# The last additions of the first two chunks of tokens: from VectorE to GpSimd

## What is computed

```python
h = h + attention(layernorm(h))
xt = layernorm(h)
shared = silu(xt @ sw1) * (xt @ sw3) @ sw2                  # one expert for every token
idx = top_k(xt @ gate_w.T + biases, 2)                       # two of eight experts for each token
p = sigmoid(top scores) / sum                                # their two weights
y = silu(xt @ w1[e]) * (xt @ w3[e]) @ w2[e]                  # for each token and chosen expert e
out = h + shared + p[0] * y[first] + p[1] * y[second]
```

## Time and profile before

| | |
|---|---|
| median of three runs | 264.31 us (263.71 to 264.48) |
| the profiled execution, whole | 264.31 us |
| its span in the profile | 262.5 us |
| busy: TensorE, VectorE, ScalarE, GpSimd | 89%, 72%, 59%, 44% |

### The profile page before, as it was taken

How to read it: one execution, slowest core, us unless ns; L and a number is a source line. 1 busy time by engine, 2 the same in 40 slices (tenths; PEclk the granted TensorE clock), 3 DMA queues, 4 the chain that set the end, 5 groups by cost and what they waited for, 6 DMA issues and landing times.

```text
span 262.5 us, 5589 instructions
## 1 busy us (share of the span) xinstructions
PE 233.8 (89%) x1491; PEld 192.2 (73%) x1491; DVE 189.9 (72%) x737; ACT 155.3 (59%) x436; POOL 115.2 (44%) x121
## 2 busy tenths in 40 slices
PE   0499799999999999989899957999999999999960
PEld 0477688888879797966566636888888888888640
DVE  1533998798989898987988767766666666665784
ACT  0325458585858585875974325666666666666571
POOL 1400000055646464640656720676666666676600
PEclk9999799999999999997999997999999999999996
DMA  6989964143434301010011412324323332348736
GB/s 199 318 271 338 333 241 149 39 122 126 117 127 121 136 21 44 20 40 2 31 42 50 135 43 52 93 62 113 85 82 91 85 98 75 99 112 236 202 99 181
DMA packets 31421, 31.68 MB, mean 121 GB/s; under 512 B 4322, under 2 KB 27403, under 8 KB 30496
## 3 DMA queue, kind: packets, MB, share of 16 engines
q1 hardware_dynamic: 25960, 23.95, 30.7%
q0 software_dynamic: 3392, 6.36, 7.4%
q10 hardware_dynamic: 2040, 1.04, 1.4%
HBM read 22.80 MB, written 9.03 MB: 121 GB/s over the span
## 4 chain that ended last, share of the span: by engine, by line
PE 80%; DVE 9%; ACT 5%; ACTq 3%; issue 2%; DVEq 0%
PE bank L1565 15%; PE bank L1281 12%; PE bank L1585 10%; PE bank L1296 5%; PE bank L1574 5%; PE bank L1488 3%; PE bank L1473 3%; PE bank L1476 3%; PE bank L1369 2%; PE bank L1556 2%; PE bank L1329 2%; PE bank L1373 2%; PE bank L1295 2%; PE bank L1327 2%; PE bank L1355 2%
## 5 line engine op out<-in xcount | busy, mean ns | idle before, releaser
L778 POOL DMA_INDIRECT xs_dram<-xd,pos_i x50 | 54.9, 1099 | 82.7 <-DVE pos_i L967 69.9
L789 POOL DMA_INDIRECT y_dram<-att,goal x56 | 56.4, 1007 | 37.7 <-ACT att L713 37.4
L1281 PE MATMUL bank<-wt,xp_both 128*128 128x128 f32 x288 | 38.6, 288 | 0.0
L1281 PEld LDWEIGHTS bank<-wt,xp_both 128*128 128x128 f32 x288 | 36.9, 201 | 1.4 <-issue 0.7
L699 ACT ACTIVATE att<-bank 128x256 f32<-128x256 f32 x56 | 21.5, 383 | 24.9 <-PE bank L1565 24.9
L1585 PE MATMUL bank<-w_sb,att 128*128 x224 | 34.5, 277 | 0.0
L1190 DVE CAST xsT_h<-bank 128x128 fp32r<-128x128 f32 x56 | 16.3, 292 | 24.9 <-PE bank L1556 24.9
L1585 PEld LDWEIGHTS bank<-w_sb,att 128*128 128x128 f32 x224 | 29.4, 191 | 0.3 <-issue 0.2
L1565 PE MATMUL bank<-xp_both,xsT_h 128*128 x56 | 27.3, 488 | 1.5 <-DVE xsT_l L1192 1.5
L1203 DVE TENSOR_TENSOR att<-att,bank 128x256 f32<-128x256 f32 x56 | 23.0, 411 | 1.6 <-ACT att L699 1.6
L1565 PE MATMUL bank<-xp_both,xsT_l 128*128 x56 | 22.6, 403 | 0.0
(11 more groups left out here) (201 smaller groups left out, 497.2 us busy)
## 6 DMA issues: line engine op xcount, KB each, us to landing
xp_both<-in_patches SPq DMA_DIRECT2D x7, 1152.0 KB, 5.2
xs_all<-xs_dram SPq DMA_DIRECT2D x56, 64.5 KB, 1.8
xd<-y_dram SPq DMA_DIRECT2D x8, 384.0 KB, 4.6
w<-in_w SPq DMA_DIRECT2D x2, 1024.0 KB, 9.7
y_dram<-att,goal POOLq DMA_INDIRECT x56, 2.3
xs_dram<-xd,pos_i POOLq DMA_INDIRECT x50
hrow<-in_txt SPq DMA_DIRECT2D x2, 384.0 KB, 10.4
out_tokens<-hrow SPq DMA_DIRECT2D x6, 128.0 KB, 1.9
```

The costliest lines, as they stand in the source:

```text
L778: nc.gpsimd.indirect_dma_start(out=xs_dram[:, :], out_offset=bass.IndirectOffsetOnAxis(ap=pos_i[0:rows, j, k:k + 1], axis=0), in_=xd[0:row ...
L789: nc.gpsimd.indirect_dma_start(out=y_dram[:, :], out_offset=bass.IndirectOffsetOnAxis(ap=goal[u][:, 0:1].bitcast(I32), axis=0), in_=ys[u][ ...
L1281: M(ps[:, 0:D], xp[p][:, k, :], wt[:, k, :], start=(k == 0), stop=False)
```

## The change

A new semaphore `fin_pool` is counted by GpSimd, which makes the plain addition of L1239 for chunks 0 and 1 at the end of its list, once `fin_first` and `scaled` allow it. The two calls `all_results(0)` and `all_results(1)` leave VectorE's list. SyncE waits for `fin_pool` before the transfers of chunks 0 and 1; the counts of `fin_done` for which SyncE and ScalarE wait are two lower for the chunks behind.

```diff
         scaled, fin_first, fin_done, out_sent = sem("scaled"), sem("fin_first"), sem("fin_done"), sem("out_sent")
+        fin_pool = sem("fin_pool")
...
         SH = G + 1
+        BY_POOL = 2
...
             for c in range(len(CHUNKS)):
-                sp.wait_ge(fin_done, c + 1)
+                if c < BY_POOL:
+                    sp.wait_ge(fin_pool, c + 1)
+                else:
+                    sp.wait_ge(fin_done, c + 1 - BY_POOL)
                 for dst, src in out_views(c)[0::(1 if c < 2 else 2)]:
                     sp.dma_start(dst, src).then_inc(out_sent, 16)
...
             for c in range(2, len(CHUNKS)):
-                act.wait_ge(fin_done, c + 1)
+                act.wait_ge(fin_done, c + 1 - BY_POOL)
...
                     in_=ys[u][:], in_offset=None, bounds_check=bound, oob_is_err=False).then_inc(y_sent[u], 16)
+            for c in range(BY_POOL):
+                a, b = CHUNKS[c]
+                pool.wait_ge(fin_first, c + 1)
+                pool.wait_ge(scaled, c + 1)
+                nc.gpsimd.tensor_tensor(hrow[:, a:b, :], hrow[:, a:b, :], y_rows[:, 1, a:b, :], ALU.add).then_inc(fin_pool, 1)
...
             shared_mul(EARLY + 1, 1)
-            all_results(0)
             dve.wait_ge(sh_add, EARLY + 1)
             first_results(3)
             shared_mul(EARLY + 2, 0)
             shared_mul(EARLY + 2, 1)
             dve.wait_ge(fin_first, 4)
             shared_add(EARLY + 1)
-            all_results(1)
             shared_add(EARLY + 2)
```

## The result

| | before | changed |
|---|---|---|
| median of 18 runs each | 264.56 us | 265.85 us |
| ratio, with its 95% interval | | 1.0053 (1.0031 to 1.0075) |
| the profiled execution, whole | 264.31 us | 267.97 us |
| its span | 262.5 us | 266.2 us |

What follows compares the result with a forecast made beforehand. The prediction took SyncE's output queue, held until chunk 1 is ready, to set the end. Its last issue would begin at 259.74 instead of 260.42, 0.68 us less: 264.31 - 0.7 gives 263.6 us, range 263.1 to 265.1.

Steps and rivals of the forecast that it cites:

- What the queue of SyncE waits for: Output transfers at the end: the moment chunk 1 is ready sets the end; up to 0.77 us can be won.
- The second limit: Output transfers at the end: nearly full transfer engines at 278 GB/s would cap the gain near 0.8 us.
- 0.5 us of closing follow. So the end is set by SyncE's queue: Program end: last transfer lands at 262.0, 0.5 us of closing follow, so SyncE's 13 output issues set the end.
- it stands idle: GpSimd after its last scatter, over at 247.44: claimed idle, with the two additions queued behind nothing.
- GpSimd's addition: Chunks 0 and 1 on GpSimd: 1.8 us each, between 1.15 and 2.11, starting at 250.25 and 253.05.
- The 0.15 us that I added for running side by side: GpSimd's second addition beside VectorE's last weighted additions: 0.15 us more, chunk 1 ready at 255.0 instead of 254.85.
- Rival 2: first_results(3) on VectorE held up by GpSimd's additions: last issue 0.75 us later, about 265.1 us; chance 0.18.
- The chances: Odds given for the whole kernel's measured time: faster 0.36, same 0.44, slower 0.20.
- VectorE's 1.7 us: Two additions leaving VectorE, 0.87 us each: most not won because of waits for ScalarE and TensorE; 0.09 us won.
- Rival 3: GpSimd's first addition costs extra: an extra of 3 us would give 265.9 us; chance 0.05 shared with another rival.
- The row by which I set the lock aside: Early VectorE operation at 10.87 beside a GpSimd copy: took 0.49 us, claimed 0.62 if held until the copy's end.

Runs made afterwards that it cites:

- the last experiment: The changed kernel, but GpSimd adds chunk 0 alone and VectorE adds chunk 1 straight after first_results(3); ratio 0.9975 (0.9945 to 1.0006) to the kernel before.

## Why the prediction was wrong

- **What the queue of SyncE waits for**: right as read. On the clock of before chunk 1's first issue came at 254.87, where 255.0 was forecast, and the last at 260.14, where 259.6 to 259.75 was. With chunk 0 alone moved, and with chunk 1 freed from the lock, the closing moved with the last issue, by 0.1 and 0.2 us. It doesn't always: in the changed kernel the last issue came 0.28 us earlier and the closing 0.17 later, and with chunk 1 earlier on VectorE they came 0.96 and 0.5 us earlier. The second limit, the transfers themselves, had been put at a gain of 0.8 us; in these runs no more than 0.5 us arrived. That it is the filled transfer engines which hold the last transfer is not shown.
- **"0.5 us of closing follow. So the end is set by SyncE's queue"** and **"it stands idle"**: the step that failed. I took GpSimd as free because its last compute row ended at 247.44, and did not ask what its list holds behind that. The drain stood in the trace of before, ending at 256.19 with 6.1 us of cover; the views of busy time, chain and timeline leave such instructions out. So the scatters are not the last that GpSimd has to do, though the description of the kernel has them so. A new end of GpSimd's work at 254.85, as I had forecast it, plus 8.75 us is 263.6, 1.3 us behind SyncE's 262.3. The missing term alone would have given 264.31 + 1.3 = 265.6 us, whatever VectorE did. The measured ratio gives 265.7 on that base.
- **GpSimd's addition**: 1.8 us taken, 1.80 and 1.83 measured; starts within 0.07 us; pick-up 0.15 us where 0.2 was taken. That the 1.8 came so near is luck in part, as it was chosen between two ends. The price for each element was too high: by the earlier trace rows a copy of 768 elements takes 1.15 us and it took 0.87 to 0.88; the second input then doubled it, which made up for that. The factor of the Trainium skill (GPSIMD Engine Reference, Performance versus the Vector engine) would have given 1.86 as an estimate, and the traces agree with it within 0.06 us. The 0.15 us that I added for running side by side did not arise on GpSimd: chunk 1 was ready at 254.84.
- **Rival 2, VectorE held up**: the mechanism was right and had been given 0.18. It named two operations held by the second addition and 1.5 us of delay; one was held, for 1.55 us, and 0.84 us arrived at shared_add(7), since there were 0.7 us of slack. Its price at the end was wrong: the 0.76 us by which chunk 2 is late fit into its 0.78 us of queueing, and SyncE's closing comes 0.17 us later than before, not 0.75. The 265.1 us it gave is near the truth for another reason.
- **The chances**: by the sentence that adds them up, rivals 2 and 3 leave 0.18 for slower and 0.46 for the same, not 0.20 and 0.44.
- **VectorE's 1.7 us won almost nothing** by waiting for ScalarE and TensorE: right. With chunk 0's addition gone there was idle time before shared_mul(8, 1), which the last experiment filled.
- **Rival 3, a dear first addition**: no sign of it. The first took 1.80 us, the second 1.83.
- **The row by which I set the lock aside was misread.** L984 began at 10.87 beside a copy that ended at 11.09, and I argued that a held operation would show 0.62 us, its own 0.40 added to the wait. But held operations of 128 elements end 0.15 us after GpSimd, and not their own 0.35: what an operation needs before its elements seems to pass during the wait. The additions of 768 and 384 elements (0.95 and 0.54 us) put an element at 1.07 ns, and 128 of them at 0.14 us. For 256 elements that makes 0.27 us: 11.09 + 0.27 = 11.36, where L984 ended. The row spoke for the lock, and the rows around it do too:

```profile
9.63 0.53 POOL L758 COPY cosx<-cst 128x256 f32<-128x256 f32 x1
...
9.93 0.50 DVE L982 TENSOR_TENSOR bq_part<-bq_in,bq_h 4x256 f32<-4x256 f32 x1
...
10.10 0.59 POOL L758 COPY cosx<-cst 128x256 f32<-128x256 f32 x1
...
11.04 0.59 POOL L758 COPY sinx<-cst 128x256 f32<-128x256 f32 x1
```

L982 ends 0.27 us after the copy that was in flight (10.43 after 10.16). And the copies that began while L982 and L984 ran took 0.59 us instead of 0.45 and ended 0.27 us after them: whichever engine begins second waits. By this reading GpSimd's scatter yielded because L873 had begun 0.15 us before it, and not because VectorE hardly yields.

## What to carry to other kernels

Work moved to an engine that "has finished" may move the program's end: look at the closing instructions of that engine (its drain), not only at its last busy row, and add its length to the new last instruction. On GpSimd, after the 106 scatters of this kernel, this is 8.75 us; give it the early part of a tail and not the last. And where GpSimd reads SBUF, count the next of VectorE's operations with two inputs in SBUF as held to the end of GpSimd's instruction, and look how much slack stands behind it before you price the delay.

## What the runs showed of the hardware

- GpSimd's closing drain takes 8.74 to 8.76 us after its last instruction with 106 scatters issued, whether that is a scatter, an addition or a write of one element, and 9.39 us with 114: by these two counts some 82 ns (an estimate) for each scatter that the program has issued, those issued over 100 us before the end among them.
- A two-input operation of VectorE that begins while GpSimd reads SBUF ends 0.15 us (for 128 elements) or 0.27 us (for 256) after GpSimd's instruction; a GpSimd write doesn't hold it. A GpSimd copy that begins while such an operation runs is held likewise (0.59 us instead of 0.45).
- GpSimd's addition of 768 elements in each partition takes 1.80 to 1.85 us, its copy 0.87 to 0.88, its write 0.74 to 0.79; VectorE's addition takes 0.94 to 0.95.
